# Gated layers of a two-layer Flamingo block: the second matrix's row as three bf16 parts, the output's residual added on VectorE, one eviction moved on ScalarE

## Time and profile before

| what | value |
| --- | --- |
| median of 3 runs | 1360.68 us (1358.73 to 1361.45) |
| time of the profiled execution | 1363.21 us |
| its span | 1361.5 us |
| PE busy (matmul) | 1096.9 us, 81% |
| DVE busy | 1038.0 us, 76% |
| ACT busy | 881.4 us, 65% |
| POOL busy | 95.0 us, 7% |
| mean granted clock of PE | 0.92 |

### The profile page before, as it was taken

One profiled execution on the slowest core, in us unless ns is written; L12 is line 12 of the kernel. 1 busy time (PEld: TensorE's weight loads), 2 busy tenths in 40 slices (PEclk: granted clock), 3 DMA queues, 4 the chain that ended last, 5 costly groups with the idle time before them and its releaser, 6 DMA issues.

```text
span 1361.5 us, 17623 instructions
## 1 busy us (share of the span) xinstructions
PE 1096.9 (81%) x5736; PEld 517.1 (38%) x5736; DVE 1038.0 (76%) x2097; ACT 881.4 (65%) x1912; POOL 95.0 (7%) x75
## 2 busy tenths in 40 slices
PE   4999994777777766766767665888999999999986
PEld 3667673101111111111111111235666766676663
DVE  2766662798888888888888886446998888888865
ACT  2232321778999999999999995564545554555542
POOL 0010113000000000000000000001011011101112
PEclk8999995556989899899998998788999999999998
DMA  7444432021211111212222101101111111110000
GB/s 226 139 163 160 142 136 53 13 32 32 41 33 36 38 22 39 40 36 40 40 41 40 31 16 48 47 8 43 54 36 35 58 41 43 36 62 20 28 20 31
DMA packets 77776, 74.89 MB, mean 55 GB/s; under 512 B 13682, under 2 KB 71284, under 8 KB 77684
## 3 DMA queue, kind: packets, MB, share of 16 engines
q1 hardware_dynamic: 77684, 73.76, 20.2%
HBM read 44.90 MB, written 28.31 MB: 54 GB/s over the span
## 4 chain that ended last, share of the span: by engine, by line
PE 38%; ACT 27%; DVE 10%; issue 6%; SPq 1%; DMA 1%; POOL 0%; DVEq 0%; ACTq 0%
ACT ea L1061 15%; PE ps_a L1275 11%; ACT prob L1069 11%; PE ps_b L1234 6%; DVE nmax L962 5%; PE ps_c L1234 4%; PE ps_v L1234 2%; PE ps_b L891 2%; PE ps_c L918 2%; PE ps_v L933 2%; PE ps_a L1255 2%; PE ps_a L891 2%; PE ps_a L1284 1%; PE ps_v L1341 1%; PE ps_c L1367 1%
## 5 line engine op out<-in xcount | busy, mean ns | idle before, releaser
L1061 ACT ACTIVATE ea<-ps_a,nmax 128x512 f32<-128x512 f32 x512 | 354.9, 719 | 49.6 <-DVE nmax L962 49.5
L962 DVE TENSOR_REDUCE nmax<-ps_a 128x2 f32<-128x1024 f32 x256 | 312.0, 1221 | 90.2 <-PE ps_a L891 89.5
L1069 ACT ACTIVATE prob<-ps_b 128x1024 f32<-128x1024 f32 x256 | 271.7, 1061 | 42.7 <-PE ps_b L891 42.7
L891 PE MATMUL ps_b<-q_st,k_st 52*128 52x512 f16 x512 | 106.0, 410 | 149.4 <-ACT prob L1069 146.8
L891 PEld LDWEIGHTS ps_b<-q_st,k_st 52*128 52x128 f16 x512 | 25.2, 93 | 383.0 <-ACT prob L1069 351.8
L1275 PE MATMUL ps_a<-wgu,xT 128*128 128x352 f32 x512 | 164.0, 465 | 2.4 <-ACT xT L1400 2.4
L918 PE MATMUL ps_c<-ea,rz 128*32 128x512 f32 x1024 | 158.3, 694 | 0.9 <-DVE rank L1005 0.9
L933 PE MATMUL ps_v<-prob,v_in 128*16 128x512 f32 x1024 | 141.6, 626 | 10.9 <-DVE att L1029 10.6
L891 PE MATMUL ps_a<-k_st,q_st 48*128 48x512 f16 x512 | 111.1, 430 | 33.4 <-ACT ea L1061 20.3
L1061 ACT ACTIVATION_READ_ACCUMULATOR ea<-ps_a,nmax 128x1 f32 x512 | 121.4, 237 | 0.0
L1275 PEld LDWEIGHTS ps_a<-wgu,xT 128*128 128x128 f32 x512 | 94.3, 191 | 49.6 <-issue 4.1
(11 more groups left out here) (234 smaller groups left out, 1621.3 us busy)
## 6 DMA issues: line engine op xcount, KB each, us to landing
q_scr<-q_p SPq DMA_DIRECT2D x24, 256.0 KB, 2.5
k_scr<-k_p SPq DMA_DIRECT2D x24, 256.0 KB, 2.5
q_st<-q_scr SPq DMA_DIRECT2D x32, 192.0 KB, 4.7
k_st<-k_scr SPq DMA_DIRECT2D x32, 192.0 KB, 5.1
mat<-m_scr SPq DMA_DIRECT2D x16, 384.0 KB, 3.1
x_in<-in_x SPq DMA_DIRECT2D x8, 512.0 KB, 6.2
c_in<-in_ctx SPq DMA_DIRECT2D x8, 512.0 KB, 4.9
v_scr<-v_s SPq DMA_DIRECT2D x8, 512.0 KB, 2.6
```

What stands on the lines that cost most here:

```text
L891: return e.matmul(bank, left[b][o:o + rows, r, t * P:t * P + P], right[b][o:o + rows, r], start=True, stop=True)
L962: e.tensor_reduce(nmax[u % 2][:, t].rearrange("p (h r) -> p r h", h=2)[:, r], ps_a[:, z % 2 * 2:z % 2 * 2 + 2], AX_X, ALU.max, negate=True ...
L1061: e.activation(ea[c % RING][:, g % 4], ps_a[:, g % 4], ACT.Exp, bias=nmax[u % 2][:, t, n:n + 1], accum_out=tot[u % 2][:, t, n:n + 1]).then ...
L1069: e.activation(prob[g % RING][:, 2 * (z % 2):2 * (z % 2) + 2], ps_b[:, :, :], ACT.Exp).then_inc(s_prob, 1)
```

## The change

In `project` the row leaves `m_s`: DVE writes it to one partition in f32, and splits it there, in five more instructions that each wait for the one before, into three bf16 rows whose sum is the f32 row. SP stores them to a scratch of their own and `feed` loads them into three partitions. In `feed` the row enters `y_ps` by one bf16 product of three rows of ones and these parts. The identity product of `r4` goes away; the bias row is then the first product into `w_ps`, and DVE adds `r4` while it evicts `w_ps` to `o_b`, at a place in its turn between x_round and variances_b. ACT's eviction of `w_ps` goes away, and gate and up eviction 3 comes after `z` and not ahead of it. All that waited for ACT's eviction now waits for DVE's. Declarations of tiles and semaphores are cut here.

```diff
@@ project, sync: store_m @@
                 e.dma_start(scr.m[b], m_s[b % 2][:, :]).then_inc(s_out_m[b % 2], 16)
+                e.dma_start(scr.r[b].unsqueeze(0), r_p[b % 2][:, :, :]).then_inc(s_out_m[b % 2], 16)
@@ project, vector: matrix_m @@
                 e.wait_ge(s_dve_mean, b + 1)
                 if b >= 2:
-                    e.wait_ge(s_out_m[p], 16 * (b // 2))
-                e.tensor_scalar(m_s[p][:, DC * D:], psE[:, 1, 0:D], mean[p][:, DC:], None, ALU.add).then_inc(s_dve_m, 1)
+                    e.wait_ge(s_out_m[p], 32 * (b // 2))
+                x, y = r_s[p], r_p[p]
+                e.tensor_scalar(x[:, 0], psE[0:1, 1, 0:D], mean[p][0:1, DC:], None, ALU.add).then_inc(*dv.up())
+                e.wait_ge(*dv.now())
+                for n in range(2):
+                    e.tensor_copy(y[:, n], x[:, n]).then_inc(*dv.up())
+                    e.wait_ge(*dv.now())
+                    e.tensor_tensor(x[:, n + 1], x[:, n], y[:, n], ALU.subtract).then_inc(*dv.up())
+                    e.wait_ge(*dv.now())
+                e.tensor_copy(y[:, 2], x[:, 2]).then_inc(s_dve_m, 1)
@@ feed, sync: turn @@
                 e.dma_start(mat[u1 % 2][:, :], scr.m[u1 // 2]).then_inc(s_ldm[u1 % 2], 16)
+                e.dma_start(mat_row[u1 % 2][:, :], scr.r[u1 // 2]).then_inc(s_ldm[u1 % 2], 16)
...
-                e.wait_ge(s_act_out, u5 + 1)
+                e.wait_ge(s_dve_out, u5 + 1)
                 e.dma_start(tokens(out[j, p * U:p * U + U]), o_b[p][:, :, :]).then_inc(s_sto[p], 16)
@@ feed, gpsimd @@
-        e.memset(one_row[:, :], 1.0).then_inc(s_set, 1)
@@ feed, tensor: first_product @@
             if u >= 6:
-                e.wait_ge(s_act_out, u - 5)
+                e.wait_ge(s_dve_out, u - 5)
@@ feed, tensor: turn @@
-                e.matmul(y_ps.rearrange("p (n d) -> p n d", n=N), one_row[:, :],
-                         mat[p][0:1, DC * D:].unsqueeze(1).to_broadcast([1, N, D]), start=True, stop=False)
+                e.matmul(y_ps.rearrange("p (n d) -> p n d", n=N), ones16[0:3, :],
+                         mat_row[p][:, :].unsqueeze(1).to_broadcast([3, N, D]), start=True, stop=False)
...
-                e.wait_ge(s_act_out, u4)
-                e.matmul(w_ps, ident[:, :], flat(r4[u4 % 3][:, :, :]), start=True, stop=False)
-                bias_row(w_ps, 1)
+                e.wait_ge(s_dve_out, u4)
+                bias_row(w_ps, 1, first=True)
@@ feed, scalar: turn @@
                 h_magnitude(u1)
-            if u5 is not None:
-                e.wait_ge(s_pe_last, u5 + 1)
-                if u5 >= 2:
-                    e.wait_ge(s_sto[u5 % 2], 16 * (u5 // 2))
-                e.activation(flat(o_b[u5 % 2][:, :, :]), w_ps, ACT.Copy).then_inc(s_act_out, 1)
             if u0 is not None:
                 x_T(u0)
-                for q in range(4):
+                for q in range(3):
                     leave(u0, q)
...
                 normal(z, pairs(y_ps), rs_b[p], nb_b[p], 1).then_inc(s_act_z, 1)
             if u0 is not None:
+                leave(u0, 3)
                 leave(u0, 4)
@@ feed, vector: turn @@
                 if u4 >= 3:
-                    e.wait_ge(s_pe_last, u4 - 2)
+                    e.wait_ge(s_dve_out, u4 - 2)
                     e.wait_ge(s_act_n4, u4 - 2)
...
                 x_round(u0)
+            if u5 is not None:
+                e.wait_ge(s_pe_last, u5 + 1)
+                if u5 >= 2:
+                    e.wait_ge(s_sto[u5 % 2], 16 * (u5 // 2))
+                e.tensor_tensor(flat(o_b[u5 % 2][:, :, :]), w_ps, flat(r4[u5 % 3][:, :, :]), ALU.add).then_inc(s_dve_out, 1)
             variances_b(i)
```

More of the change, by code:

```diff
@@ L112, in __init__ @@
         self.v = dram("v_scr", [B, P, TT, D], F32)
-        self.m = dram("m_scr", [B, P, DC * D + D], F32)
+        self.m = dram("m_scr", [B, P, DC * D], F32)
+        self.r = dram("r_scr", [B, 3, D], BF16)
         self.c = dram("c_scr", [DC, B, P, T], F32)
@@ L434, in project @@
         q_p, k_p = m.two("q_p", [P, 2, DC, T], F16), m.two("k_p", [P, 2, DC, T], F16)
-        v_s, m_s = m.two("v_s", [P, TT, D]), m.two("m_s", [P, DC * D + D])
+        v_s, m_s = m.two("v_s", [P, TT, D]), m.two("m_s", [P, DC * D])
+        r_s, r_p = m.two("r_s", [1, 3, D]), m.two("r_p", [1, 3, D], BF16)
         gram, x1, rb = m.two("gram", [P, DC, D]), m.two("x1", [P, DC, D]), m.two("rb", [P, D])
@@ L494, in _ @@
                 e.wait_ge(s_out[p], 16 * 7 * B // 2)
-                e.wait_ge(s_out_m[p], 16 * B // 2)
+                e.wait_ge(s_out_m[p], 32 * B // 2)
         @block.tensor
@@ L1118, in feed @@
     x_in, att = m.two("x3_in", [P, N, D]), m.two("att3", [P, DC, U])
-    mat = m.two("mat", [P, DC * D + D])
+    mat, mat_row = m.two("mat", [P, DC * D]), m.two("mat_row", [3, D], BF16)
     r1 = [m.sb(f"r1{n}", [P, N, D]) for n in range(3)]
@@ L1126, in feed @@
     tm, half = m.sb("tm3", [P, 2, N]), m.sb("half", [P, 2, N])
-    one_row, ones16 = m.sb("one_row", [1, P]), m.sb("ones16", [65, P], BF16)
+    ones16 = m.sb("ones16", [65, P], BF16)
     bias16 = m.sb("bias16", [65, 2, D], BF16)
@@ L1160, in feed @@
         m.sem(f"pe_{n}3") for n in ("wo", "xT", "sum", "down", "decT", "y", "q8T", "last"))
-    (s_act_xn, s_act_xm, s_act_xT, s_act_hm, s_act_dec, s_act_decT, s_act_sq, s_act_z, s_act_n4, s_act_q8T,
-     s_act_out) = (m.sem(f"act_{n}3") for n in (
-         "xn", "xm", "xT", "hm", "dec", "decT", "sq", "z", "n4", "q8T", "out"))
+    (s_act_xn, s_act_xm, s_act_xT, s_act_hm, s_act_dec, s_act_decT, s_act_sq, s_act_z, s_act_n4, s_act_q8T) = (
+        m.sem(f"act_{n}3") for n in ("xn", "xm", "xT", "hm", "dec", "decT", "sq", "z", "n4", "q8T"))
     (s_dve_r1, s_dve_st1, s_dve_xq, s_dve_x, s_dve_hid, s_dve_hq, s_dve_h, s_dve_st2, s_dve_rb, s_dve_zg, s_dve_r4,
-     s_dve_q) = (m.sem(f"dve_{n}3") for n in (
-         "r1", "st1", "xq", "x", "hid", "hq", "h", "st2", "rb", "zg", "r4", "q"))
+     s_dve_q, s_dve_out) = (m.sem(f"dve_{n}3") for n in (
+         "r1", "st1", "xq", "x", "hid", "hq", "h", "st2", "rb", "zg", "r4", "q", "out"))
     s_pe_gu, s_act_gu = m.sem("pe_gu3"), m.sem("act_gu3")
@@ L1216, in gpsimd @@
         e.memset(mv_b[:, :, :, 1], 1.0).then_inc(s_set, 1)
-        e.wait_ge(s_set, 7)
+        e.wait_ge(s_set, 6)
         for i in range(TURNS):
@@ L1335, in turn @@
                 p = u2 % 2
-                e.wait_ge(s_ldm[p], 16 * (u2 // 2 + 1))
+                e.wait_ge(s_ldm[p], 32 * (u2 // 2 + 1))
                 if u2 == 0:
```

## The result

The kernel became slower, by about what was forecast: 14.6 us by the medians, 12.5 us between the two profiled executions, for a forecast of 13.0. The changed kernel takes 1375.54 us (median of 6 runs, 1371.05 to 1378.94), the kernel before 1360.99 us (6 runs, 1358.73 to 1365.13). The ratio is 1.0103, with a 95% interval of 1.0080 to 1.0126. The forecast was 1373.7 us, with a range of 1364 to 1380. The profiled execution has a span of 1374.0 us and a time of 1375.67 us, where the sum of the prediction gave 1376.2.

The account below looks back on a forecast made before the run. The prediction took PE as the bound, with project a closed loop through DVE's c1w. Project's delay 12.2, its clock 7.5 and feed -6.7 gave +13.0 us on 1360.7, so 1373.7 us, range 1364 to 1380.

Parts of the forecast that it names:

- The delay in project: Project: five added DVE instructions, 1.9 us ahead of c1w, delay seven matrix_x1 starts and the end; +12.2 us (9.3 to 18).
- The last wait: Project's end: PE waits for DVE after the last matrix_m, 0.4 of 1.9 us hidden; +1.5 us.
- The clock in project: Project: longer PE idle ahead of matrix_x1 brings five clock falls at 1.5 us each; +7.5 us (0 to 12).
- Feed's full turns: Feed: PE sheds work, a turn falls from 27.10 to 25.46 us, PE stays the bound; -20.2 us in sum.
- DVE's vanished wait: Feed, turns 2 to 4, where DVE is nearly always busy: its wait goes away, a gain of 0.4 us.
- The halves: Feed turn on PE: f32 row product 1.05 us becomes bf16 0.22; identity product 0.96 goes, DVE's eviction adds 0.09.
- ACT's move: Feed: z ahead of eviction 3 readies zg over 1 us earlier, worth nothing by itself, only keeps 0.4 us.
- The drain: Feed from turn 16 on: DVE's eviction waits for PE's last product and delays the statistics chain; +13.5 us (9 to 16).
- The waits behind the eviction: Drain: variances_b, power and roots_b queue behind DVE's eviction; +2.7, +2.5, +2.4 in turns 16 to 18, then +4.1 us.
- Rival 1: Project: PE's clock stays up, so only 12.2 - 6.7 counts; 1366 us, chance 0.17.
- Rival 2: Project: c1w is not on the loop, only first start and last wait pay; 1357 or 1350 us, chance 0.09.
- Rivals 3 and 4: Feed: DVE bounds full turns, 1380 us, chance 0.07; three-row bf16 product lasts as long as f32, 1384 us, 0.02.

Follow-up runs that it names:

- experiment 5: Changed kernel, but from turn 16 on DVE evicts the output behind its roots and roundings; 1356.9 us, ratio 0.9973 to the kernel before.
- experiment 10: Changed kernel with the later drain evictions, the split on GpSimd behind its FP4 products, and the row's store a batch later; 1341.2 us, ratio 0.9852 to before.
- experiment 6: Changed kernel with two unused f32 identity products put into PE's idle time ahead of matrix_x1; 1371.9 us, ratio 1.0071 to the kernel before.
- experiment 1: Kernel before with the row part of the change alone, ACT still evicting and PE still adding the residual; 1370.1 us, ratio 1.0049 to before.
- experiment 3: Changed kernel with ACT's gate and up eviction 3 ahead of z again; 1373.7 us, ratio 1.0092 to the kernel before.
- experiment 9: Changed kernel with the row split into two bf16 parts instead of three, the third part zero; 1367.4 us, ratio 1.0045 to the kernel before.
- experiment 8: Changed kernel with the split on GpSimd ahead of its FP4 products and DVE's drain evictions behind its roots; 1345.4 us, ratio 0.9877 to the kernel before.
- experiment 4: Changed kernel with the split's five instructions moved later on DVE, behind c1w and ahead of the q parts; 1371.4 us, ratio 1.0078 to the kernel before.
- experiment 7: Changed kernel with the split's five instructions on GpSimd, behind c1w and ahead of its FP4 products; 1362.5 us, ratio 1.0002 to the kernel before.

## Why the prediction was right

Forecast and mechanism held. That the span was hit within 0.5 us is luck, for two reasons. Two terms were off in opposite directions: project was put 4.8 us too high at x_T of turn 2, the drain 3.5 us too low. And the profiled execution had four clock falls in project's loop, where the same code in experiment 5 had one; other executions of the changed kernel took from 1371 to 1379 us.

**The delay in project (predicted +12.2 us, found +11.6).** The steps were right one by one. The kernel of experiment 5, with one fall only, shows them bare: its periods are 1.8, 3.1 (a fall of 1.7 among it), 1.8, 1.8, 1.8, 1.5 and 0.3 us longer than before, counted from the first matrix_x1; without the fall that is 10.2 us, predicted were 1.9, 1.5, 1.8, 1.8, 1.8, 1.5 and 0.35. The last wait was put at +1.5: from the last matrix_x1 to the FP4 transposes it is 12.16 us there, against 10.78 in experiment 10, where no split stands on DVE, +1.4.

**The clock in project (predicted +7.5 us, found +6.0).** Right in mechanism, too large in sum. The changed kernel's four falls in the loop cost 1.7, 1.5, 1.7 and 1.5 us (its periods less those without a fall in experiments 5 and 6), 6.4 in all, where five at 1.5 were predicted. Its last stretch had a fall too, 13.46 us for 12.16. But the profiled execution of before had one there as well, behind idle times of 1.51, 1.30 and 1.16 us, which the prediction overlooked: its sentence that gaps up to 1.5 us in project left the clock up is wrong. The timeline of before, PE, at the end of project:
```profile
209.56 0.79 PE L542 MATMUL psE<-kvs,wq 128*128 128x128 f32 x2 [1.16 <-DVE kvs L645]
210.15 0.64 PE L545 MATMUL psE<-ident 128*128 128x128 f32 x2
```
The same identity products take 0.39 us at 2.4 GHz (209.76 in the changed kernel), and the stretch took 12.52 us for experiment 10's 10.78. So the clock cost 6.4 + 1.3 - 1.7 = 6.0 us more than before, and 11.6 + 6.0 is the 17.5 by which the way to the FP4 transposes grew, within 0.1. What the forecast took as sure for each gap came only part of the time, and what decides it stays open: over the changed kernel and experiments 1, 3 and 5, 12 of the 21 idle times of 2.9 us were followed by a fall, and of those of 2.0 to 2.1 us, experiment 9 included, 3 of 8. Of the idle times of up to 1.8 us ahead of matrix_x1 none was followed by a fall within these products, in any kernel. One fall of experiment 3 was longer and cost 3.0 us (97.59 to 124.50, 26.91 us for 23.93). The Trainium skill, TensorE: Matmul & The Clock Gate, section "Why this matters for your kernels", which warns only of longer idle gaps, would have made this term 0; these starts and the filled gap of experiment 6 speak against it here.

**What was not seen.** No term held the clock of the FP4 transposes. Before, all of them ran at 1.2 GHz (1.6 us for six with `gq`); after, part of them ran at 2.4 GHz (0.97 us for six). The first product of attend comes 13 us behind the last of them. The timeline of before, PE:
```profile
237.59 1.03 PE L891 MATMUL ps_a<-k_st,q_st 48*128 48x512 f16 x4 [12.94 <-DMA k_st<-k_scr]
```
The timeline after the change, PE:
```profile
253.01 1.03 PE L902 MATMUL ps_a<-k_st,q_st 48*128 48x512 f16 x4 [12.79 <-DMA k_st<-k_scr]
```
From the first FP4 transposes to this product it is 19.38 us for 21.95. So of the 18.0 us by which they started late, 2.6 were regained there and 0.6 on the way from it to x_T of turn 2 (699.99 us for 700.55), which leaves 14.9. It is no gain of the change: in experiments 3 and 5, with the project of the changed kernel, all these transposes ran at 1.2 GHz and the first stretch took 22.2 and 21.8 us. The prediction carried project's whole delay, 19.7 us, to the end. Of the 4.8 us by which it was off at x_T of turn 2, 3.1 were lost here and 2.1 in the two terms above; the first matrix_x1 itself came 0.5 us later. The second stretch, nearly all of it code that is the same everywhere, took 696.4 to 702.7 us in the twelve profiles; the forecast had no term for that.

**Feed's full turns (predicted -18.5 between the landmarks, found -17.7).** A turn came down by 1.59 us for a predicted 1.64, ten of them give 15.9, turn 4 gives 1.7 as predicted. DVE's vanished wait of 0.4 gave 0.14 in turns 2 and 3. The halves were right: the row's product gives 0.73, identity product and eviction 0.86 (predicted 0.77 and 0.87). DVE was ready in time by the 0.5 us that stand ahead of its eviction (predicted 0.44). The reading of the earlier trace rows was loose: two slices of feed are below 9 tenths at its end, 8 and 6, and not one; the sum doesn't use it. That ACT's move is worth nothing was right (experiment 3).

**The drain (predicted +11.8 with turns 15 and 16, found +15.3).** By landmarks (`z` of turn 16, of 17, of 18, the end), each from the one before:

| from, to | before | after | difference | predicted |
| --- | --- | --- | --- | --- |
| x_T of 15, `z` of 16 | 28.25 | 30.53 | +2.3 | 2.7 - 0.9 - 0.8 = +1.0 |
| to `z` of 17 | 18.78 | 21.37 | +2.6 | +2.5 |
| to `z` of 18 | 11.19 | 14.13 | +2.9 | +2.4 |
| to the end | 18.45 | 25.98 | +7.5 | 4.1 + 0.1 and clock |

The waits behind the eviction were right to 0.5 us in each turn: in turn 16 from the start of matrix M's product to `z` it is 16.66 us for 14.02, +2.64 for the predicted 2.7, and in the last turns from the start of the eviction to the transposes of q8 it is 5.28 us for 0.39, the predicted +4.9. Too much was credited to turns 15 and 16, 1.7 us of which 0.4 came. And the clock was put at +1.7 in all: in the last two turns alone the products take 3.78 us for 1.93 and 1.89 and the transposes of the last turn 1.11 for 0.66, together 4.2 us. The prediction let PE start at the lower clock and priced it at 0.9 us for the last turn; PE kept the lower clock to the end of both products. That is the term that was mis-sized. The eviction's place is the cause of all of it: experiment 5 moves nothing else and gets 16 us back.

**The rivals.** Rival 1 (clock stays up) is out by the rows and by experiment 6. Rival 2 (`c1w` not on the loop), the other side, is out: all seven starts are released by `c1w`, and moving the split off DVE's hand-over (experiment 10) brings every period back, with the FP4 transposes as early as before. Rivals 3 and 4 are out: turns of 25.51 us, and a bf16 product of 0.39 us.

## What to carry to other kernels

Work that leaves the bounding engine is gained at the pace of the steady loop, but what takes its place must be followed through every stage and through the end of the pipeline. Here a gain of 17.7 us was worth keeping and was eaten by five tiny instructions on one partition ahead of a hand-over, and by one wait that stood ahead of a chain which only the drain hangs on. The wait was repaired by order alone, the five instructions by moving them to GpSimd, and there too the order counted (experiments 8 and 10). When instructions are moved away, look first at what runs on GpSimd at the new place: an instruction of 0.28 us moved beside a GpSimd product cost 2.63.

## What the runs showed of the hardware

- The same idle time of 2.90 us on PE, in the same code, is followed by a clock fall in some batches and not in others, 12 times in 21, and one fall costs 1.5 to 1.7 us, once 3.0. Whether the falls spread the times is not shown: the changed kernel spreads over 7.9 us in 6 runs and experiment 10, without such gaps, over 3.6 us in 4, but the kernel before, without them too, over 6.4 us in 6.
- Filling an idle time of PE with products that nothing uses took the falls away and brought the FP4 transposes 6.1 us forward (experiment 6; the medians, 3.6 us apart, are within the noise).
- Casts, subtractions and products of DVE on SBUF alone lasted until the GpSimd product beside them ended, even on one partition (experiments 4 and 7), and GpSimd's small instructions are slowed by DVE in turn: a cast of 0.39 us took 1.8 us beside DVE's FP4 rounding, as the rows of GpSimd in experiment 7's first batch show:
```profile
70.82 1.78 POOL L770 CAST r_p<-r_s 1x256 bf16<-1x256 f32 x1 [50.47 <-DVE c1w L695]
72.69 1.26 POOL L772 TENSOR_TENSOR r_s<-r_s,r_p 1x256 f32<-1x256 f32 x1
```
